# Decoder layer on one core: the loads of the prologue in pieces and in another order, rope tables in two parts

## The reference, cut to what matters

```
def reference(x, ctx, w_qkv, w_o, qn_g, qn_b, kn_g, kn_b, ...):      # x: (16, 100, 512)
    h = layernorm(x)
    qkv = h @ w_qkv.T            # 16 query heads, 4 key heads, 4 value heads of 128
    q, k, v = split(qkv)
    q = layernorm(q, qn_g, qn_b)          # over the 128 of a head
    k = layernorm(k, kn_g, kn_b)
    q = q * cos + rotate_half(q) * sin    # rope: position tables of 100 x 128
    k = k * cos + rotate_half(k) * sin
    x = x + (softmax(causal(q @ k.T / sqrt(128))) @ v) @ w_o.T
    x = x + cross_attention(layernorm(x), ctx, ...)    # 32 heads of 16, 361 context rows
    x = x + ffn(layernorm(x), ternary(W_up), ternary(W_gate), ternary(W_down))
    return x
```

## Time and profile before

| | |
|---|---|
| median of 3 runs | 1402.93 us (1398.98 to 1403.82) |
| the profiled execution | 1401.41 us |
| its span, first to last instruction | 1399.3 us |
| mean granted TensorE clock | 0.984 |
| TensorE busy | 1315.0 us, 94% |
| VectorE busy | 780.1 us, 56% |
| GpSimd busy | 274.1 us, 20% |
| start of the first matmul | 9.87 us |
| start of `project(0, 0)` | 31.49 us |

### The profile page before, as it was taken

How to read it: one execution, slowest core, us unless ns; L and a number is a source line. 1 busy time by engine, 2 the same in 40 slices (tenths; PEclk the granted TensorE clock), 3 DMA queues, 4 the chain that set the end, 5 groups by cost and what they waited for, 6 DMA issues and landing times.

```text
span 1399.3 us, 27527 instructions
## 1 busy us (share of the span) xinstructions
PE 1315.0 (94%) x10968; PEld 868.8 (62%) x10968; DVE 780.1 (56%) x1938; ACT 641.5 (46%) x1452; POOL 274.1 (20%) x266
## 2 busy tenths in 40 slices
PE   4779999999999999999999999999999789999996
PEld 4656666666666666566666666666666445565543
DVE  3888775777677774534345444444345885444422
ACT  1443334333443335356666666666667222232321
POOL 0335441444444441211111112111111000000000
PEclk8989999999999999999999999999999999999999
DMA  8400000000000002011211111111213420000000
GB/s 258 143 25 1 1 1 1 1 1 2 1 1 1 1 1 112 22 68 49 70 61 46 45 45 45 45 45 46 66 47 122 155 87 23 0 23 1 22 1 28
DMA packets 22418, 59.99 MB, mean 43 GB/s; under 512 B 1177, under 2 KB 9369, under 8 KB 19091
## 3 DMA queue, kind: packets, MB, share of 16 engines
q1 hardware_dynamic: 22291, 58.24, 12.6%
HBM read 54.96 MB, written 3.28 MB: 42 GB/s over the span
## 4 chain that ended last, share of the span: by engine, by line
PE 83%; DVE 6%; issue 3%; ACT 1%; DVEq 0%; ACTq 0%
PE A L1592 21%; PE A L1505 11%; PE C L1914 10%; PE A L1559 10%; PE C L1616 6%; PE B L1633 5%; PE C L1545 3%; PE C L1530 3%; PE A L1930 2%; PE B L1930 2%; PE A L1514 2%; PE B L1601 2%; PE B L1538 2%; PE B L1522 2%; DVE qk L1113 1%
## 5 line engine op out<-in xcount | busy, mean ns | idle before, releaser
L1592 PE MATMUL A<-wxhl,arena 128*122 128x512 f16 x1152 | 265.3, 380 | 0.0
L1592 PEld LDWEIGHTS A<-wxhl,arena 128*122 128x122 f16 x1152 | 149.1, 134 | 88.0 <-issue 8.3
L1914 PE MATMUL C<-arena 128*128 128x375 f16 (+1 forms) x1024 | 185.9, 334 | 3.8 <-DVE arena L1114 3.8
L1505 PE MATMUL A<-arena,wxhl 128*125 128x512 f16 (+1 forms) x780 | 175.9, 383 | 6.8 <-DVE tub L953 5.0
L1914 PEld LDWEIGHTS C<-arena 128*128 128x128 bf16 x1024 | 99.6, 98 | 80.1 <-issue 6.4
L499 POOL TENSOR_TENSOR arena<-arena,region 100x512 f32<-100x512 f32 (+1 forms) x64 | 66.0, 1064 | 422.8 <-DVE region L1077 422.8
L1505 PEld LDWEIGHTS A<-arena,wxhl 128*125 128x125 f16 (+1 forms) x780 | 105.4, 137 | 66.9 <-DVE tub L953 5.4
L683 ACT ACTIVATE arena<-C 122x1600 f32<-122x1600 f32 x96 | 144.3, 1504 | 4.4 <-PE C L1616 2.8
L475 POOL TENSOR_TENSOR region<-tub 125x512 f32<-125x512 f32 (+1 forms) x65 | 82.6, 1271 | 277.4 <-DVE tub L953 277.3
L611 ACT ACTIVATE region<-C,negm 100x100 f32<-100x100 f32 x256 | 84.4, 356 | 102.2 <-DVE negm L997 102.2
L1559 PE MATMUL A<-arena,stageb 128*125 128x512 f16 (+1 forms) x416 | 123.8, 379 | 0.7 <-ACT arena L667 0.7
(11 more groups left out here) (163 smaller groups left out, 2092.4 us busy)
## 6 DMA issues: line engine op xcount, KB each, us to landing
stageb<-in_wffn SPq DMA_DIRECT2D x16, 768.0 KB, 4.7
arena<-in_ctxt SPq DMA_DIRECT2D x16, 722.0 KB, 4.7
stageb<-in_wffn SPq DMA_DIRECT2D x6, 1024.0 KB, 4.7
wxhl<-in_wffn SPq DMA_DIRECT2D x6, 1024.0 KB, 4.8
arena<-in_wqkv SPq DMA_DIRECT2D x4, 1024.0 KB, 22.4
arena<-in_wx SPq DMA_DIRECT2D x3, 1024.0 KB, 7.0
out_x<-xres SPq DMA_DIRECT2D x12, 250.0 KB
xres<-in_x SPq DMA_DIRECT2D x1, 2250.0 KB
```

Source lines behind the costliest of these rows:

```text
L1505: ins = pe.matmul(A[j % 2][0:m, :], xp[:, k, at:at + m], wp[:, j, k, :], start=(n == 0), stop=(n == 11))
L1592: ins = pe.matmul(A[(par + n) % 2][0:rows, :], lhs, wp[:, 0 if n == 0 else 1 if n < 4 else 2, k, :], start=(i == 0), stop=(i == 11))
L1914: ins = pe.matmul(C[2 * (e % 2) + half][:, 0:cols], wf[:, 3 * (e // 4) + half, k, (e % 4) * 128:(e % 4 + 1) * 128], part[:, k, 0:cols], st ...
```

## The change

The constants are laid out anew, so that the identity and the centring matrix stand first and come in one load of 256 columns; the rest (cosines and sines by column, mask and others) is a second load, with a semaphore of its own. Weight tile 0 is loaded in two halves of 256 columns, each with a semaphore; `centre` is split in halves, and TensorE does `centre(0, 0)`, `x_turn(0)`, `centre(0, 1)`; ScalarE and VectorE follow in the same order. Gains and the first quarter of the rope table are loaded behind weight tile 1, the rest of the constants and the bias columns behind tile 2, the other three quarters of the rope table behind tile 5. Gains and rope lie in another buffer (`region3` in place of `tub`), since they now live on while `tub` is used. The products of gains and rope are made for one quarter ahead of the loop (`tables(slice(0, 1))`) and for the other three behind `normed(1)` (`tables(slice(1, 4))`); the instructions for `ropeC` are moved behind `proj(0, 1)` (`columns`).

```diff
-C_ID, C_COST, C_SINT, C_MASK, C_ONE, C_PAR, C_CEN, C_END = 0, 128, 228, 328, 428, 431, 433, 561
+C_ID, C_CEN, C_COST, C_SINT, C_MASK, C_ONE, C_PAR, C_END = 0, 128, 256, 356, 456, 556, 559, 561
...
             sp.dma_start(xres[:, 0, :], xt[:, 0, :]).then_inc(ld_x0, 16)
-            sp.dma_start(cst[:], consts).then_inc(ld_c, 16)
-            for j in range(6):
+            sp.dma_start(cst[:, 0:C_COST], consts[:, 0:C_COST]).then_inc(ld_c, 16)
+            w0 = staged(0)[0]
+            sp.dma_start(w0[:, :, 0:256], wqkv[:, 0, :, 0:256]).then_inc(ld_half, 16)
+            sp.dma_start(w0[:, :, 256:512], wqkv[:, 0, :, 256:512]).then_inc(ld_w[0], 16)
+            for j in range(1, 6):
                 dst, loaded, _ = staged(j)
                 sp.dma_start(dst, wqkv[:, j]).then_inc(loaded, 16)
-                if j == 0:
+                if j == 1:
                     sp.dma_start(gain, gains).then_inc(ld_g, 16)
-                    sp.dma_start(cossin, rope).then_inc(ld_g, 16)
-                    sp.dma_start(bcol[:], bcols).then_inc(ld_g, 16)
+                    sp.dma_start(cossin[:, 0], rope[:, 0]).then_inc(ld_g, 16)
+                elif j == 2:
+                    sp.dma_start(cst[:, C_COST:C_END], consts[:, C_COST:C_END]).then_inc(ld_c2, 16)
+                    sp.dma_start(bcol[:], bcols).then_inc(ld_b, 16)
+            sp.dma_start(cossin[:, 1:4], rope[:, 1:4]).then_inc(ld_r, 16)
...
+            w_centred(0, 0)
             x_hi(0, A[1])
-            for half in range(2):
-                w_centred(0, half)
+            w_centred(0, 1)
...
             normed(0, rs1[:, 0:1])
-            x_lo(0, A[1])
-            dve.wait_ge(ld_c, 16)
-            dve.wait_ge(ld_g, 48)
-            for w, g in ((0, 2), (1, 0)):
-                dve.tensor_tensor(ropeA[:, w], gain[:, g * D:(g + 1) * D].unsqueeze(1).broadcast_to([TW, 4, D]),
-                                  cossin[:, :, 0:D], ALU.mult).then_inc(d_tab, 1)
...
-            dve.wait_ge(d_tab, 6)
+            def tables(t):
+                for w, g in ((0, 2), (1, 0)):
+                    n = t.stop - t.start
+                    dve.tensor_tensor(ropeA[:, w, t], gain[:, g * D:(g + 1) * D].unsqueeze(1).broadcast_to([TW, n, D]),
+                                      cossin[:, t, 0:D], ALU.mult).then_inc(d_tab, 1)
+                    dve.tensor_tensor(ropeB[:, w, t], gain[:, (g + 1) * D:(g + 2) * D].unsqueeze(1).broadcast_to([TW, n, D]),
+                                      cossin[:, t, D:2 * D], ALU.mult).then_inc(d_tab, 1)
+            def columns():
+                dve.wait_ge(ld_c2, 16)
+                dve.wait_ge(ld_b, 16)
+                for w, g in ((0, 2), (1, 0)):
+                    st.chain(dve.tensor_scalar(ropeC[:, w], cst[:, C_COST:C_COST + S], bcol[:, g:g + 1], None, ALU.mult))
+                    dve.scalar_tensor_tensor(ropeC[:, w], cst[:, C_SINT:C_SINT + S], bcol[:, g + 1:g + 2],
+                                             ropeC[:, w], ALU.mult, ALU.add).then_inc(d_tab, 1)
...
-            for half in range(2):
-                w_centred_lo(0, half)
+            w_centred_lo(0, 0)
+            x_lo(0, A[1])
+            w_centred_lo(0, 1)
+            dve.wait_ge(ld_g, 32)
+            tables(slice(0, 1))
+            dve.wait_ge(d_tab, 4)
             for j in range(5):
                 if j < 4:
                     for half in range(2):
                         w_centred_lo(j + 1, half)
                 proj(0, j)
+                if j == 1:
+                    columns()
...
             head_norm(0)
             normed(1, rstd[:, 20:21])
+            dve.wait_ge(ld_r, 16)
+            tables(slice(1, 4))
+            dve.wait_ge(d_tab, 10)
             z_back(0, 0, B[0])
...
             pe.wait_ge(ld_c, 16)
+            centre(0, 0)
             x_turn(0, A[1])
-            centre(0)
+            centre(0, 1)
             for j in range(5):
                 if j < 4:
-                    centre(j + 1)
+                    for half in range(2):
+                        centre(j + 1, half)
```

More of the change, by code:

```diff
@@ L266, in build @@
         carve = carver(tub)
-        cossin = carve([TW, 4, 2 * D])
-        gain = carve([TW, 4 * D])
-        carve = carver(tub)
         x2h = carve([128, KT, 4 * TW], F16)
@@ L275, in build @@
         pr = carve([S, H * S])
+        carve = carver(region3)
+        cossin = carve([TW, 4, 2 * D])
+        gain = carve([TW, 4 * D])
         carve = carver(region3)
@@ L331, in build @@
         C = [Call[:, i * 512:(i + 1) * 512] for i in range(4)]
-        ld_c = sem("ld_c")
+        ld_c, ld_c2 = sem("ld_c"), sem("ld_c2")
+        ld_half, ld_r, ld_b = sem("ld_half"), sem("ld_r"), sem("ld_b")
         ld_g = sem("ld_g")
@@ L1478, in _, with centre @@
             ident = cst[0:128, C_ID:C_ID + 128]
-            def centre(j):
+            def centre(j, half):
                 src, loaded, n = staged(j)
-                pe.wait_ge(loaded, n)
-                for half in range(2):
-                    if j > 0:
-                        pe.wait_ge(d_cen, 2 * (j - 1) + half + 1)
-                    for k in (2 * half, 2 * half + 1):
-                        for h in range(4):
-                            ins = pe.matmul(C[k][:, h * D:(h + 1) * D], src[:, h, k * 128:(k + 1) * 128],
-                                            cst[:, C_CEN:C_CEN + D], start=True, stop=True)
-                    ins.then_inc(pe_cen, 1)
+                if j == 0 and half == 0:
+                    pe.wait_ge(ld_half, 16)
+                else:
+                    pe.wait_ge(loaded, n)
+                if j > 0:
+                    pe.wait_ge(d_cen, 2 * (j - 1) + half + 1)
+                for k in (2 * half, 2 * half + 1):
+                    for h in range(4):
+                        ins = pe.matmul(C[k][:, h * D:(h + 1) * D], src[:, h, k * 128:(k + 1) * 128],
+                                        cst[:, C_CEN:C_CEN + D], start=True, stop=True)
+                ins.then_inc(pe_cen, 1)
             def x_turn(i, bank):
```

## The result

The changed kernel takes 1391.72 us (median of 7 runs, 1388.72 to 1393.44). The kernel before, run beside it, takes 1399.12 (7 runs, 1398.87 to 1403.82). The ratio over the runs is 0.992, with a 95% interval of 0.9906 to 0.9934: 9 to 13 us less, 11.2 in the middle. The two medians are only 7.4 us apart, since the one of before fell among its lower runs (1398.87 to 1399.12) and the one of the changed kernel among its upper ones (1391.72 to 1393.44). A second comparison with the same kernel gave 1391.88 against 1401.85, ratio 0.9927 (0.9914 to 0.9939). The profiled execution took 1391.79 us (span 1389.7), 9.6 us less than the profiled one of before. Forecast were 8.4 us.

The account below looks back on a forecast made before the run. TensorE, busy for 94% of the span, was taken as the bound, with the start of its steady work at 31.49 us to move. 12.8 - 0.3 - 4.1 = 8.4 us off 1402.93 gave 1394.5 us, range 1389.5 to 1398.5.

Parts of the forecast that it names:

- the restart: TensorE's next start after the gap, at 86.77 us before the change; the moved products' whole cost was to reach it.
- moved table products: Four products behind normed(1), expected to take turns with GpSimd's scalings: cost 4.1 us, bounds 0 and 4.1.
- The front: From the first loads to project(0, 0): start at 18.7 instead of 31.49 us, 12.8 us earlier, ends 12.0 and 13.8.
- columns(): Four small VectorE instructions behind proj(0, 1), partly waiting beside GpSimd's w_of: cost 0.3 us, bounds 0 and 2.2.
- Rival 1: Moved products behind normed(1): VectorE pays one wait of 1.04 us or none; saving 11.5 to 12.5 us; chance 0.33.
- Rival 2: Load queue: tiles beside gains and rope stay slow, TensorE waits 2 us for tile 2; saving 6.4 us; chance 0.12.
- Rival 3: First load of weight tile 0: the half completes only at 9.7 us; saving 5.6 us; chance 0.07.
- Rival 4: Weight tile 0 in 1 KB pieces loads more slowly: kernel slower, at about 1412 us; chance 0.03.
- both of its places: normed(1) at 1.37 us beside GpSimd's scalings; a GpSimd product at 2.90 us beside a long VectorE subtraction at 90.00 us.

Follow-up runs that it names:

- none: Changed kernel without the four moved products, first rope quarter read for every tile (later positions wrong): 1386.12 us, ratio 0.9889.
- quiet: Changed kernel with GpSimd's five scalings of tile 0 held back until the four moved products are done: 1392.61 us, ratio 0.993.
- whole: Changed kernel with weight tile 0 in one load instead of two halves: 1393.88 us, ratio 0.9943.
- gap: Changed kernel with the four moved products behind w_lo(8), gains and rope in a buffer of their own: 1389.41 us, ratio 0.9908.
- gap_rows: As gap, with gains and rope stored and loaded as 128 rows and x tile 0 as 120 and 5 rows: 1385.93 us, ratio 0.9887.
- rows2: The kernel of gap_rows unchanged, run again in the next comparison: 1387.31 us, ratio 0.9893.

## Why the prediction was off, point by point

The time of 1391.72 us lies in the range, and the sign and each mechanism came as forecast. What failed is the sum: 12.8 - 0.3 - 4.1 = 8.4 us measured 13.6 - 0.0 - 3.2 = 10.4 at the restart. The step with the largest error is the price of the moved table products, put at 4.1 us, four turns of 1.54; it is 3.2 us, four turns of 1.31. The front was put 0.8 us too low, `columns()` 0.3 too high, and one term was missing: the clock behind the restart, which gives another 0.9 us. With it the lead is 11.3 us, and the ratio says 11.2. The two medians by themselves are 7.4 us apart; that this is near 8.4 is luck.

- **The front: 12.8 forecast, 13.6 measured.** The first matmul was forecast at 7.7 and came at 7.49: 0.2 us. `centre(0, 0)` at half clock, `x_turn` at 0.8 (0.73) and the thirty-two matmuls behind it at 4.1 (4.12) were right. The rest is hand-overs: I set each group behind the full duration of the one before, but in the timeline consecutive groups on TensorE overlap by 0.1 to 0.2 us, and VectorE's hand-over cost 0.29 us instead of 0.5.
- **`columns()`: 0.3 forecast, 0.0 measured.** The wait beside GpSimd came (0.7 us) and was hidden entirely.
- **The moved products: 4.1 forecast, 3.2 measured** (3.0 by `none`). This is the largest error of the three terms. That they take turns was right, and `quiet` shows it by taking the cause away. A turn was put at one scaling and one product, 1.04 + 0.5 = 1.54 us; it is 1.31. Four times 0.23 are the 0.9 us. By themselves, in `quiet`, a product takes 0.47 us (the step between two starts) and a scaling 1.01 (5.03 for five), so inside a turn the product adds only 0.3 to a scaling.
- **The clock behind the restart: not in the sum, 0.9 us.** The prediction held that all of the stage's saving reaches the restart at 86.77 us and stopped there. In the ten microseconds behind it the granted clock is 0.84 in the changed kernel and 0.74 in the one before, and the lead grows from 10.4 to 11.3 us.
- **The base.** I took the 8.4 us off 1402.93, a median of three runs. The seven runs of the comparison have 1399.12, since four of them fall into a lower group. In the later comparisons the runs of the kernel before lie at 1398.5 to 1399.2 us with a mean clock of 0.987 (one with 0.985), at 1400.9 to 1402.2 with 0.984, and at 1402.3 to 1405.4 with 0.981 or 0.982. The forecast time against the new median is a change of 0.33%, against the old one 0.60%. The profiled run (1401.41, clock 0.984) would have been the better base: it is the one run whose parts I had, and with the measured 10.4 it gives 1391.0.
- **Rival 1 (one wait or none)** had nearly the size (1390.4 to 1391.4), for the wrong reason: the products waited each time.
- **Rival 2 (the queue)** didn't come. Tile 2 landed at 19.5 us (forecast 19.8), and TensorE didn't wait for it. The price of a row count was in it, though: the rope quarter came at 17.2 (forecast 17.4), with a wait of 1.34 us where I had put under 1. The argument that made this rival less likely was weak: it put 375 KB at 2.6 us, estimated from the figure that the prediction cites, while the rope quarter landed 4.7 us after tile 1. By the same estimate the 750 KB of before are 5.2 us and not 10.5, so the prediction's "that agrees with the 10.5 us" holds for the direction only. Five engines are shown, by the semaphore increments; why they took twice the estimate isn't.
- **Rival 3 (no early half)** fell at once, with the first matmul at 7.49, and `whole` puts a price on the half, 1.6 us. **Rival 4 (1 KB pieces)** fell too: by the one profile of `whole`, 1024 such pieces are about 0.3 us slower than 128 rows of 8 KB.

The rule of the Trainium skill that the prediction weighed ("SBUF — State Buffer", section "Who interferes with whom") held for the products: a VectorE instruction with two SBUF inputs contends with a GpSimd instruction that reads SBUF, for ports that are locked exclusively. It doesn't give the length of a turn. An exclusion over the whole of both instructions, as the prediction read it, would make 1.5 us of a turn, and 1.31 was measured. The prediction also said that the trace agrees with this rule at both of its places. `normed(1)` is not a case of it, since it reads one SBUF tensor and two values per row; that it is long beside GpSimd is shown by `quiet` alone, 0.55 us against 1.36.

What stays open: why the product is cheaper inside a turn than alone, why one of sixteen shares of the first half came 1.2 us after the others in `gap`, with the same loads ahead of it, and why the five shares behind the 125-row loads took 10.5 us. What in the later work makes the clock fall in one run and not in another isn't shown either.

## What to carry to other kernels

When a small load holds back a queue for longer than its bytes explain, look at its number of rows before its place: 128 rows instead of 125 gave here what a new order of everything gave. Work that is moved into a hole of one engine has to be checked against what the neighbour engine does in that hole; the same four instructions cost 3 us beside GpSimd and 0.1 some 18 us later. And with effects below 1%, compare marks inside the trace (first projection, restart) before medians: the marks of one program repeated to 0.7 us here, while the medians of the kernel before lay between 1399.1 and 1402.8 us. Take one mark more behind the last wait, since the clock there can add to the lead (0.9 us here).

## What the runs showed of the hardware

- **Rows of a load.** Gains, rope and bias columns (752 KB in all) held back the next tile by 10.5 us with 125 rows in the first two, by 2.0 with 128. A load of 125 rows raises its semaphore by five late increments, one of 128 by sixteen. `x` tile 0 lands at 3.7 us as 120 and 5 rows, at 5.5 as 125. The busy share of the DMA engines reads full (1.02) at 243 GB/s and at 426.
- **A series beside a series.** VectorE products of two SBUF operands (0.47 us each by themselves) beside GpSimd scalings (1.01 us each by themselves) alternate at 1.31 us a turn, and even a single-input `normed(1)` takes 1.36 us instead of 0.55.
- **The clock.** It rose at a different moment after the first matmul in two profiles of one program (`x_turn` took 0.59 us in `gap_rows` and 1.04 in `rows2`), and later it falls in places that differ from profile to profile; one such place cost 1.7 us of the lead. The runs of the kernel before fall into groups some 2 to 4 us apart, each with a mean clock of its own (0.987, 0.984, 0.981 to 0.982).
